# Spline cells repeated through DRAM scratch instead of by sixteen on-chip copies, in a fused convolution and spline kernel

## The reference

```python
out = relu(batchnorm(conv3x3(x, sign(w1)), gamma1, beta1))
out = batchnorm(conv3x3(out, sign(w2)), gamma2, beta2)
x = relu(out + x)

x_aff = clip(x * a + b, -1.5, 1.5)              # per channel
u = (x_aff + 1.0) * 0.5 * (K - 1)               # K = 32
i = floor(u); t = clip(u - i, 0, 1)
spline = alpha_table[clip(i-1)] * b0(t) + alpha_table[clip(i)] * b1(t) \
       + alpha_table[clip(i+1)] * b2(t) + alpha_table[clip(i+2)] * b3(t)   # R = 8 columns, b0..b3 cubic
y_nl = einsum('bchwr,cr->bchw', spline, mix)
out = id_gain * x + y_nl + bias
```

## Time and profile before

| | us |
|---|---|
| median of three runs | 1382.41 |
| profiled execution | 1388.55 |
| its span, first to last instruction | 1386.8 |
| TensorE busy (matmuls) | 1266.2 |
| VectorE busy | 999.2 |
| ScalarE busy | 914.0 |
| spline matmuls (line 975) | 868.8 |
| sign masks (line 808) | 529.0 |

### The profile page before, as it was taken

One profiled execution on the slowest core, in us unless ns is written; L12 is line 12 of the kernel. 1 busy time (PEld: TensorE's weight loads), 2 busy tenths in 40 slices (PEclk: granted clock), 3 DMA queues, 4 the chain that ended last, 5 costly groups with the idle time before them and its releaser, 6 DMA issues.

```text
span 1386.8 us, 63578 instructions
## 1 busy us (share of the span) xinstructions
PE 1266.2 (91%) x29706; PEld 840.6 (61%) x29706; DVE 999.2 (72%) x917; ACT 914.0 (66%) x360; POOL 56.2 (4%) x116
## 2 busy tenths in 40 slices
PE   6899994999995299999989989999999998999997
PEld 4677772688883056556556656656655665666564
DVE  5666655666666277888788878887787878887875
ACT  4344434678872577768776777667776887687770
POOL 4000000560000000000000000000000000000000
PEclk9999997999998599999999999999999999999999
DMA  6577655577764433553445443543445344534321
GB/s 226 213 278 271 259 212 192 202 275 281 260 260 186 139 116 121 169 157 123 142 132 180 137 142 122 183 145 119 142 162 158 129 142 153 175 122 142 119 73 49
DMA packets 53520, 236.10 MB, mean 170 GB/s; under 512 B 15808, under 2 KB 15808, under 8 KB 45248
## 3 DMA queue, kind: packets, MB, share of 16 engines
q1 hardware_dynamic: 41024, 207.08, 41.2%
q10 hardware_dynamic: 12288, 25.71, 7.0%
HBM read 104.29 MB, written 77.07 MB: 131 GB/s over the span
## 4 chain that ended last, share of the span: by engine, by line
ACT 18%; PE 17%; issue 13%; ACTq 9%; DMA 5%; DVE 4%; SPq 0%; DVEq 0%
PE tab L975 17%; ACT mask L808 11%; ACTq L794 8%; DMA cell<-cell 5%; ACT zbuf L775 3%; ACT cell L783 2%; ACT side L802 2%; DVE poly L908 1%; DVE poly L895 1%; DVE poly L914 1%; DVE lin L857 0%; DVE mask L874 0%; DVE offset L866 0%; SPq L744 0%; DVE poly L901 0%
## 5 line engine op out<-in xcount | busy, mean ns | idle before, releaser
L975 PE MATMUL tab<-mask,diag 128*32 128x392 bf16 x20480 | 868.8, 332 | 67.4 <-DVE mask L874 22.2
L975 PEld LDWEIGHTS tab<-mask,diag 128*32 128x32 f16 x20480 | 538.2, 98 | 397.7 <-issue 28.6
L808 ACT ACTIVATE mask<-cell,thr 128x6272 bf16<-128x6272 bf16 x96 | 529.0, 5513 | 231.6 <-issue 195.1
L633 PE MATMUL acc<-band_split,w 64*64 64x392 f16 x4608 | 197.9, 330 | 16.0 <-DVE band_split L425 13.3
L633 PE MATMUL acc<-split,w 64*64 64x392 f16 x4608 | 197.6, 331 | 14.9 <-DVE split L436 11.1
L908 DVE SCALAR_TENSOR_TENSOR poly<-tab,first,poly 128x1568 f32<-128x1568 f32 x96 | 177.7, 1851 | 42.5 <-PE tab L975 35.1
L352 ACT ACTIVATE yout<-acc 128x1568 f32<-128x1568 f32 x64 | 94.3, 1473 | 172.5 <-PE acc L633 172.5
L633 PEld LDWEIGHTS acc<-band_split,w 64*64 64x64 f16 x4608 | 159.1, 107 | 54.6 <-issue 20.2
L445 DVE BATCH_NORM_STATS2 stats<-yout 128x392 f32 (+1 forms) x256 | 126.0, 555 | 89.1 <-ACT yout L352 88.2
L633 PEld LDWEIGHTS acc<-split,w 64*64 64x64 f16 x4608 | 141.7, 107 | 70.2 <-issue 16.0
L914 DVE SCALAR_TENSOR_TENSOR poly<-offset,poly 128x1568 f32<-128x1568 int32 x64 | 114.7, 1792 | 2.2
(11 more groups left out here) (103 smaller groups left out, 371.0 us busy)
## 6 DMA issues: line engine op xcount, KB each, us to landing
y_scratch<-yout SPq DMA_DIRECT2D x32, 1568.0 KB, 6.2
xin<-y_scratch SPq DMA_DIRECT2D x16, 1568.0 KB, 9.0
zbuf<-y_scratch SPq DMA_DIRECT2D x32, 784.0 KB, 4.4
lin<-in_x SPq DMA_DIRECT2D x32, 784.0 KB, 6.1
cell<-cell SPq DMA_DIRECT2D x256, 98.0 KB, 3.1
cell<-cell ACTq DMA_DIRECT2D x256, 98.0 KB, 3.3
out<-lin SPq DMA_DIRECT2D x32, 784.0 KB, 4.7
xin<-in_x SPq DMA_DIRECT2D x15, 1568.0 KB, 9.3
```

Of the source, the lines that this page charges most:

```text
L633: mm = pe.matmul(acc[h * C:(h + 1) * C, 2 * k + r, 0:TILE], weights[part][own, tap * C:(tap + 1) * C], image[own, first:first + ROWS, dx:d ...
L808: act.activation(mask[b % 2][q][:, :, :], cell4[b % 2][:, :, :], ACT.Sign, bias=thr[:, q:q + 1]).then_inc(sign_mask_ready, 1)
L975: mm = pe.matmul(tab[(b + t) % 2][j * GROUP:(j + 1) * GROUP, sub, 0:SUB], keep["diag"][part][:, j % 2, t, q, :], mask[b % 2][q][:, j, sub ...
```

## The change

The cell numbers go to a new DRAM tensor `cell_scratch` of two slots. SP stores the 128 rows of a chunk with one transfer, waits until it has landed (`cell_parked`), and issues four loads, one for each j: rows j*32 to j*32+31 of the slot, read four times over, fill all 128 partitions of `cell4[:, j, :]`. ScalarE issues no transfers any more. In ScalarE's turn, the position now comes ahead of the first mask, and the cells between the first and the second.

For chunk 0 all four masks are made by VectorE (`first_masks`): 0 or 1 for quad 0, 0 or 2 for the sign quads, with the base value `plain`, which doesn't hold the half sum. ScalarE makes no mask of chunk 0. In ScalarE's and VectorE's opening the cells and the offsets of chunk 0 come earlier. TensorE's 32 chunks are written out without a loop; the other engines keep their loops.

```diff
+            def by_group(s, j):
+                return parked[s][j * GROUP:(j + 1) * GROUP, :].rearrange("(o c) x -> o c x", o=1).broadcast_to((4, GROUP, CHUNK))
             def spread(i, b):
...
                 sp.wait_ge(cell_ready, made)
                 wait_past(sp, mask_ready, used)
                 wait_past(sp, sign_mask_ready, used_signs)
-                for g in range(2):
-                    for j in range(4):
-                        sp.dma_start(cell4[b % 2][g * GROUP:(g + 1) * GROUP, j, :],
-                                     cell[b % 2][j * GROUP:(j + 1) * GROUP, :]).then_inc(copied[b % 2], 16)
+                sp.dma_start(parked[b % 2], cell[b % 2][:, :]).then_inc(cell_parked, 16)
+                sp.wait_ge(cell_parked, parked_by_now)
+                for j in range(4):
+                    sp.dma_start(cell4[b % 2][:, j, :], by_group(b % 2, j)).then_inc(copied[b % 2], 16)
...
             position(0, 0)
+            cells(0, 0)
             position(0, 1)
-            cells(0, 0)
-            spread(0, 0)
-            sign_mask(0, 0, SIGN_QUADS[0])
-            sign_mask(0, 0, SIGN_QUADS[1])
             cells(0, 1)
-            spread(0, 1)
-            sign_mask(0, 0, SIGN_QUADS[2])
             sides(0, 0)
...
+            def first_masks():
+                dve.wait_ge(copied[0], COPIES)
+                for q in range(QUADS):
+                    dve.tensor_scalar(mask[0][q][:, :, :], cell4[0][:, :, :], keep["above"][:, q:q + 1],
+                                      2.0 if q in SIGN_QUADS else 1.0, ALU.is_ge, ALU.mult).then_inc(mask_ready, 1)
...
-            rounds(pe, body)
+            for i in range(CHUNKS // BUFS):
+                for b in range(BUFS):
+                    body(i, b, i)
...
+        parked = nc.dram_tensor("cell_scratch", (2, P, CHUNK), BF16).ap()
```

More of the change, by code:

```diff
@@ L48 @@
 BUFS = 4
+COPIES = 64
 SHIFT = 192.0
@@ L540, in spline_constants @@
                 link(dve.tensor_tensor(t, t, col(INV_AMP), ALU.mult), tail)
-                first = keep["first"][:, T_VAL:T_VAL + 1]
-                dve.tensor_tensor(first, first, t, ALU.add).then_inc(spline_ready, 1)
-                dve.wait_ge(spline_ready, 1)
+                for name in ("first", "plain"):
+                    first = keep[name][:, T_VAL:T_VAL + 1]
+                    dve.tensor_tensor(first, first, t, ALU.add).then_inc(spline_ready, 1)
+                dve.wait_ge(spline_ready, 2)
             def norm(conv, s, gamma):
@@ L653, in _, with spline @@
                 pe.matmul(ps_small[:, 96:98], avg[:, :], mv[:, :], start=True, stop=True).then_inc(mean_ready, 1)
-def spline(nc, sem, keep, y2, x, out):
+def spline(nc, sem, keep, parked, y2, x, out):
     with ExitStack() as ctx:
@@ L712, in rounds, with vector_masks, sign_masks @@
             four(last, last)
+        def vector_masks(c):
+            return (c + 1) * len(VECTOR_QUADS) + len(SIGN_QUADS) if not isinstance(c, int) or c >= 0 else 0
+        def sign_masks(c):
+            return c * len(SIGN_QUADS) if not isinstance(c, int) or c >= 0 else 0
         def exists(n, b):
@@ L823, in body @@
                 following, after = exists(n, b + 1), exists(n, b + 2)
+                if after:
+                    position(i, b + 2)
                 if following:
@@ L826, in body @@
                 if after:
-                    position(i, b + 2)
+                    cells(i, b + 2)
                 if following:
                     sign_mask(i, b + 1, SIGN_QUADS[1])
-                if after:
-                    cells(i, b + 2)
-                    spread(i, b + 2)
-                if following:
                     sign_mask(i, b + 1, SIGN_QUADS[2])
@@ L875, in masks, with base @@
                                       ALU.is_ge).then_inc(mask_ready, 1)
-            def base(t):
-                return first[:, t:t + 1]
+            def first_masks():
[3 more added lines that the diff above has]
+                                      2.0 if q in SIGN_QUADS else 1.0, ALU.is_ge, ALU.mult).then_inc(mask_ready, 1)
+            def base(i, b, t):
+                start = keep["plain"] if isinstance(i, int) and i == 0 and b == 0 else first
+                return start[:, t:t + 1]
             def used(i, b, t):
@@ L886, in side_product @@
                 dve.wait_ge(table_ready, used(i, b, T_ABS))
-                dve.scalar_tensor_tensor(out=quarters(side), in0=summed(i, b, T_ABS), scalar=base(T_ABS),
+                dve.scalar_tensor_tensor(out=quarters(side), in0=summed(i, b, T_ABS), scalar=base(i, b, T_ABS),
                                          in1=quarters(side), op0=ALU.add, op1=ALU.mult).then_inc(table_used, 1)
@@ L926, in _ @@
             fixed(0, 0)
+            offsets(0, 0)
             linear(0, 0)
-            offsets(0, 0)
             fixed(0, 1)
             linear(0, 1)
-            masks(0, 0)
+            first_masks()
             def body(i, b, n):
```

43 lines of the change are left out of this document (21 added, 22 removed).

## The result

The changed kernel takes **1490.82 us** (median of 4 runs, 1487.31 to 1492.42), against 1382.09 us for the kernel before on the same chip: ratio 1.0781, 95% interval 1.0756 to 1.0806. The change makes it 7.8% slower. I had forecast 1403 us: the sign was right, the size was not, +21 us against +109 us. The profiled span is 1488.0 us.

A forecast was written before the change was run, and what follows sets the result against it. It took the copy ring to bound the changed kernel at 28.7 us a chunk: chunk 31's copy at 1360.5 plus 46.7 us, span 1407.4 with an extra instruction, 1409.2 with 1.75 around, times 0.9956: 1403 us; range 1360 to 1530.

The forecast's parts named there:

- The ring: Spline, each chunk: mask, cell, store and loads follow one another and bound the kernel, 28.7 us a turn against 28.08.
- Four engines for a load: Cell loads: an outermost repeat of 4 splits each into 4 parts of 32 rows on the same four DMA engines.
- the loads' time: Four cell loads of a chunk: 16.5 us of rows plus 2.5 us fixed, 19.0 us; bounds 17.0 and 26.4.
- so they mostly fit: z, x and output rows, 5.9 us on the same four engines, mostly fit into 7 us between copy and next store.
- The row price: Cell store and loads: 129 ns per 3136-byte row, from a straight line through two lone stores' row lengths.
- Store: SP's store of a chunk's cells to DRAM: 8 x 0.129 + 1.4 = 2.4 us, bounds 2.3 and 4.2.
- Mask and cell: ScalarE's part of a turn: 5.51 + 1.59 = 7.1 us, 7.4 with hand-overs, less 0.1.
- each 0.1 us of the turn is 3 us: Spline: every 0.1 us in the turn of a chunk changes the kernel's time by 3 us.
- The rival of slower rows: Cell loads on four engines at 150 ns a row: turn 31.4 us, 1484 us; at 160 ns 1523 us. Chance 0.14.
- Opening masks worth 0: Chunk 0's masks by VectorE gain 0, since chunk 1's copy is on the path; up to 7 us slower is covered.
- The loop: TensorE's chunks written out: saves 2.6 to 3.0 us at each of five turns, but hidden by TensorE's wait.
- The rival "sixteen engines": Cell loads shared by all sixteen engines take 6.6 us, ring 16.3 us, TensorE bounds: 1323 us. Chance 0.15.

The follow-up runs named there:

- Cut by rows: Changed kernel with its four loads cut into one per group of 32 partitions, 32 outermost in source and destination: 1387.36 us, ratio 1.0027.
- one-at-a-time kernel: Changed kernel, but SP waits for each of the four loads to land before issuing the next: 1817.13 us, ratio 1.3143.
- kernel with distinct rows: Changed kernel, but each load reads four different stretches of 32 rows instead of the same 32 rows four times: 1471.28 us, ratio 1.0645.
- rows written long ago: Changed kernel, but from chunk 2 on stores go to two further scratch slots while loads keep reading the first two: 1489.72 us, ratio 1.0745.
- the version with sixteen SBUF copies: Changed kernel with the earlier kernel's sixteen SBUF-to-SBUF copies, all issued by SP, instead of the way through DRAM scratch: 1327.13 us, ratio 0.9603.

## Why the prediction was right in sign and wrong in size

The measured time lies inside the wide range (1360 to 1530 us) and above the range of the forecast itself (1388 to 1470 us).

**The ring** (mask, cell, store, wait, four loads) was right, and so was its place as the bound: 27 waits of ScalarE for the copy in 27 chunks.

**Four engines for a load** was right. The page says under 512 B 8640 packets, before 15808. Without the sixteen copies' 512 x 16 closing packets 7616 are left; 32 x 16 for the stores and 128 x 4 for the loads make 8640 exactly. Cut by rows, there are 10176 of them, 128 x 12 more. This was the rule of the Trainium skill, "DMA: Bandwidth & Descriptors", section "Rules for kernel authors", that a leading broadcast of c copies confines the transfer to at most c engines; the trace agrees, 25.8% of sixteen engines in use from 708 to 714 us.

**The term that failed is the loads' time**, "I take 2.5: loads 19.0 us", and with it the overlap, "so they mostly fit". From the issues and masks of 26 turns it is 21.4 us on average, median 21.0. The row price was even a little high. The DMA answer of the changed kernel for 712 to 722 us:

```profile
GB/s 100 88 113 100 100 100 100 100 100 100 100 100 351 376 426 427 426 376 376 401 163 133 191 100 100 113 100 100 100 100 100 100 100 100 100 100 113 226 276 163
```

Outside the stretch with the output store it stands at 100 GB/s: 3136 bytes in 125 ns an engine, where I had 129. But from 706 to 712 us:

```profile
DMA packets 129, 0.41 MB, mean 69 GB/s; under 512 B 2, under 2 KB 2, under 8 KB 128
```

The first 128 rows take 6 us instead of 4. 128 x 0.125 = 16.0 us, so what lies around the rows is 5.4 us on average and not the 2.5 that I read from a z load on sixteen engines, with only eight rows on each. The slow start is 2 us of it; the one-at-a-time kernel shows it apart, 7.5 us for 4.0 us of rows.

The other part is an overlap that I had put at nothing. The prediction has the rows of z, x and the output on the same four engines, and sends them into the 7 us between one copy and the next store. SP's list, for the loads issued at 705.89 and landed at 726.50, shows where they go:

```profile
714.28 0.36 SPq L769 DMA_DIRECT2D out<-lin  x1
720.39 0.35 SPq L743 DMA_DIRECT2D zbuf<-y_scratch  x1
```

In every turn the output store follows the loads by 5 to 9 us and z by 13 to 16 us, into the midst of them; only x falls into the gap. At the prediction's 245 ns a row their eight rows each would be 3.9 us an engine, an estimate. The last two turns, which have no z any more, show its part: their loads take 21.29 and 18.89 us here, 18.94 and 18.86 in the kernel with distinct rows (mean 20.6 before), 19.55 and 19.26 in the one with rows written long ago (mean 21.6). That is 1.7 to 2.5 us less in five of the six. No run left the output store or z out of the other turns, so the two shares are not measured apart.

Reading the same rows four times costs 0.66 us of a turn. In three of the 26 turns the loads took 24.7 to 24.9 us; with distinct rows none took more than 22.3, so part of the 0.66 may be theirs; what marks these three is open.

**Store**: 2.4 forecast, 2.86 on average between the issues. **Mask and cell**: 7.3 forecast, 7.05 measured.

The sum of the turn is then 7.05 + 2.86 + 21.4 = 31.3 us (31.15 over all thirty) against 28.7. Of the 80.6 us by which the span was missed (1488.0 - 1407.4), 30 x 2.45 = 73.5 are this (over all thirty turns the loads' mean is 21.24 us); 6.5 us are chunk 1's copy, there at 505.98 instead of 499.5. The sentence "each 0.1 us of the turn is 3 us" was the one to heed: 2.5 us from sixteen-engine rows was a thin base for a term multiplied by 30. The rival of slower rows had the size (1484 us), at a chance of 0.14. One of its reasons, that z and x share the four engines, is borne out by z; its 150 ns a row is not.

**The opening.** The copy of chunk 0 lets VectorE start its masks at 477.16, where I had 475.9; before it was 463.22. Chunk 1's copy was late as worked out, and more: its store had landed at 481.94 instead of 480.4, and its loads, with z and x behind them at 491.6 and 492.0, took 24.0 us instead of 19.0. SP's list from 455 to 467 us shows a thing that I had not expected:

```profile
457.67 8.13 SPq L745 DMA_DIRECT2D lin<-in_x  x1
```

Issuing one transfer took 8.13 us, where it mostly takes 0.33, so the store of chunk 1 was issued at 465.84. What that costs isn't shown: chunk 0's loads held the four engines until 477.16 in any case, and the store landed 4.8 us after them. "Opening masks worth 0" is right for the changed kernel in substance: TensorE stops for 7.5 us before chunk 0's last table (511.48 us) in any case, since VectorE stands before it at the mask of chunk 1 and waits for that copy until 505.98. With TensorE as the bound they are worth about 11 us.

```profile
477.16 7.14 DVE L881 TENSOR_SCALAR mask<-cell,above 128x6272 bf16<-128x6272 bf16 x4 [21.78 <-DMA cell<-cell_scratch]
```

The second operation costs nothing: 1.79 us a mask.

**The loop** was hidden as said: written out in the kernel before, it gave nothing (ratio 1.0013).

**The rival "sixteen engines"** was priced at 1323 us, and its experiment gave 1387. The price of the ring and of the 41.6 ns matmuls was right; the version with sixteen SBUF copies reaches 1327 by the same sum. Missing was the instruction supply: I had counted the load's 6 us as hidden, and TensorE waits about 1.8 us a chunk behind it.

Where the gain of the change went: the new order, ScalarE's freedom, the loop written out and the opening masks are together worth 4.0%; the detour through DRAM on four engines takes 31.15 - 26.63 = 4.5 us a chunk and turns it into a loss of 7.8%. These 4.5 us make 136 of the 162 us between the two spans (1488.0 and 1326.1); the rest lies in the opening and at the end.

## What to carry to other kernels

Before a transfer goes into a ring that every chunk passes, look at what stands outermost in both access patterns: a repeat of 4 in front of 32 rows put this one on four engines and made it more than three times as long. A fixed part read from a transfer over all engines doesn't hold for one confined to a few; with thirty turns behind it, price it from both sides. Look also at what the issuing engine's list puts behind a long transfer: the output store and z, issued into the midst of the loads, shared their four engines. And large transfers handed over together, which fill all DMA engines, are not free for an engine that runs on fresh instructions: if it waits for "issue" at the same place of every chunk, look for its instruction packets beside the transfers just before, and break the burst up.

## What the runs showed of the hardware

- TensorE's instruction packets come late behind a burst of four 392 KB loads issued within 1.8 us and spread over all sixteen DMA engines: 42.1 us of stops in 24 chunks with one burst, 4.2 with two, none with a quarter of the bytes. With sixteen 98 KB copies issued over 12 us there are none either, though the engines are full for up to 8 us at a time. The Trainium skill, "Runtime: NRT & Kernel Launch", section "Instruction fetch mechanics", says that the cost of fetching the next block of straight-line code is mostly hidden. In the last two kernels it is; behind the burst it isn't, and there the measurement decides.
- A turn of the loop costs TensorE 3.7 us on average where it is the bound; in one turn it was 4.1, of which 2.3 show as a gap.
- On four engines: 125 ns for 3136 bytes, 63 ns for 1568, but no more than 16 GB/s an engine with rows of 12544 bytes; a load on idle engines brings its first 32 rows an engine at about 160 ns.
- SP was held for 8.13 us by the issue of one transfer while the loads of chunk 0 stood on the four engines; the output store's issue, 5 to 9 us behind later loads, took 0.3 to 2.4 us. Only the place suggests the loads' backlog as the cause; no run took it apart.
